# A decoder of six sub-layers on one core: one block of denominators added by GpSimd, other orders in three stages, a split ending

## What is computed

```
x = ln(x + differential_attention(x))     # 16 heads in pairs, out1 - lambda * out2, causal
x = ln(x + long_convolution(x, ctx, ctx)) # 32 groups of 8 channels, filter as long as the sequence
x = ln(x + experts(x))                    # top 2 of 8
x = ln(x + attention(x))                  # "P": plain, 16 heads of 32, causal
x = ln(x + cross_attention(x, ctx))       # "C": one head, keys are the context and x
x = ln(x + shared_key_attention(x))       # "H" then "A": 16 heads, one shared key and value
```

## Time and profile before

| | us |
|---|---|
| three runs | 2245.63, 2247.85, 2248.08 (median 2247.85) |
| the profiled execution | 2249.93 |
| its span (first to last instruction) | 2248.10 |
| PE busy | 2099.8 (93% of the span) |
| DVE busy | 1248.4 (56%) |
| POOL busy | 546.9 (24%) |

### The profile page before, as it was taken

One profiled execution on the slowest core, in us unless ns is written; L12 is line 12 of the kernel. 1 busy time (PEld: TensorE's weight loads), 2 busy tenths in 40 slices (PEclk: granted clock), 3 DMA queues, 4 the chain that ended last, 5 costly groups with the idle time before them and its releaser, 6 DMA issues. The chain is left out here.

```text
span 2248.1 us, 29336 instructions
## 1 busy us (share of the span) xinstructions
PE 2099.8 (93%) x11903; PEld 1226.3 (55%) x11903; DVE 1248.4 (56%) x1886; ACT 517.0 (23%) x783; POOL 546.9 (24%) x514
## 2 busy tenths in 40 slices
PE   6899999888999899899999879999999999999996
PEld 4444444333444466565565646566666666666653
DVE  2467777666999944022222234355757585847465
ACT  1444444440000121111111111222222222222221
POOL 2122222227777400011111310212221212111122
PEclk9999999989999999999999989999999999999997
DMA  9850000005111045412221520101010101010000
GB/s 175 98 41 29 29 29 20 31 19 193 41 41 48 28 145 213 171 66 66 66 66 60 202 76 29 48 1 48 1 57 1 57 1 38 1 29 10 1 10 20
DMA packets 65634, 129.58 MB, mean 58 GB/s; under 512 B 6400, under 2 KB 19840, under 8 KB 65504
## 3 DMA queue, kind: packets, MB, share of 16 engines
q1 hardware_dynamic: 44848, 75.39, 13.3%
q10 hardware_dynamic: 14976, 33.69, 4.1%
q0 software_dynamic: 5680, 18.62, 2.8%
HBM read 96.36 MB, written 41.81 MB: 61 GB/s over the span
## 5 line engine op out<-in xcount | busy, mean ns | idle before, releaser
L930 PE MATMUL conv_conv<-kv,toep 128*128 128x512 f32 x576 | 248.6, 594 | 0.0
L2267 DVE RECIPROCAL tail_inv<-tail_ring 128x256 f32<-128x256 f32 x64 | 112.4, 1757 | 179.8 <-PE tail_ring L1729 179.6
L1428 PE MATMUL moe_gu_ps<-gu,moe_xT 128*128 x624 | 199.8, 463 | 3.9 <-issue 2.3
L930 PEld LDWEIGHTS conv_conv<-kv,toep 128*128 128x128 f32 x576 | 108.7, 191 | 140.5 <-issue 124.4
L953 POOL TENSOR_TENSOR kv<-vT,cT 128x512 f32<-128x512 f32 x128 | 147.8, 1176 | 57.7 <-PE conv_conv L930 53.1
L1428 PEld LDWEIGHTS moe_gu_ps<-gu,moe_xT 128*128 128x128 f32 x624 | 116.4, 192 | 73.2 <-issue 24.2
L2012 POOL TENSOR_TENSOR tail_rstd_x<-tail_rstd_x,const_minus_half 128x2 f32<-128x2 f32 x32 | 22.6, 708 | 481.5 <-DVE tail_rstd_x L2219 481.5
L2019 POOL TENSOR_SCALAR_AFFINE_SELECT tail_expT<-tail_expT 128x1024 f32<-128x1024 f32 x64 | 71.2, 1113 | 276.0 <-ACT tail_expT L2089 275.3
L540 POOL TENSOR_SCALAR_AFFINE_SELECT front_expT<-front_expT 128x2048 f32<-128x2048 f32 x32 | 64.4, 2013 | 259.9 <-ACT front_expT L598 259.9
L1512 DVE TENSOR_TENSOR moe_hid<-moe_gu_ps,moe_silu 128x352 f32<-128x352 f32 x39 | 20.5, 525 | 180.0 <-PE moe_gu_ps L1428 180.0
L2089 ACT ACTIVATE tail_expT<-tail_scores 128x1536 f32<-128x1536 f32 x64 | 92.9, 1451 | 74.6 <-PE tail_scores L1707 74.6
(11 more groups left out here) (349 smaller groups left out, 3968.3 us busy)
## 6 DMA issues: line engine op xcount, KB each, us to landing
toep<-toeplitz SPq DMA_DIRECT2D x32, 320.0 KB, 2.9
y_slots<-moe_y ACTq DMA_DIRECT2D x39, 256.0 KB, 2.0
gu<-in_L_ffn_gate_up_proj SPq DMA_DIRECT2D x5, 1408.0 KB, 10.5
toeplitz<-filt_rows SPq DMA_DIRECT2D x1, 6144.0 KB, 67.1
front_e<-in_ctx SPq DMA_DIRECT2D x8, 512.0 KB, 5.9
toeplitz<-filt_rows SPq DMA_DIRECT2D x2, 2048.0 KB, 88.2
x_after<-x SPq DMA_DIRECT2D x8, 512.0 KB, 5.0
tail_x<-x_after SPq DMA_DIRECT2D x8, 512.0 KB, 3.7
```

Source lines behind the costliest of these rows:

```text
L930: ins = pe.matmul(bank, toep[p][:, mat * P:(mat + 1) * P], kv[p][:, c].rearrange("p b j i -> p (b j i)"), start=n == 0, stop=n == len(PART ...
L1428: ins = pe.matmul(gu_ps[:, s % 2, h, 0:HID], xT[:, c, :], wgu[c][:, e, h * HID:(h + 1) * HID], start=c == 0, stop=c == NC - 1)
L2267: link.after(dve.reciprocal(inv[c % 2][:], bank[:, S:2 * S]))
```

## The change

It has five parts.

1. First stage, denominators: for f = 0 to 6 GpSimd adds the exponentials of key blocks n = 4 and n = 5 into block 5 (`sum_keys`, 128x2048 f32, in place), once O(f, 1, 1) has been computed from them, and Z(f, 1, 1) then has 4 matmuls instead of 8 and waits for this sum.
2. First stage, order: value(d) moves ahead of score(a, 3), Z and the context's transposes behind it, square_sums(f, 1) behind score(a, 5), on VectorE combine(f, 1, 1) behind maxima(a, 3). Round 1 (a = 0) gets an order of its own, with a projection behind each score block. The four loads of `wo` move on ScalarE's queue behind take_value(0).
3. Convolution: the products of two blocks lie side by side, and one `sums` adds both (64 reductions instead of 128).
4. Tail, rounds 0 and 1: written out by hand on TensorE, ScalarE and VectorE, with own query, key and value buffers for sequence 1, and projections and score blocks alternating.
5. Tail, end: for the last A GpSimd adds no blocks (TensorE takes all three), and rows t = 0 and t = 1 are added, normalised and stored one after the other.

```diff
+        def summed_keys(b, ab, t):
+            return ab == t == 1 and b < B - 1
...
                     for name in names:
+                        one = name == "Z" and summed_keys(b, ab, t)
+                        if one:
+                            pe.wait_ge(keys_summed, b + 1)
                         bank = ring.claim(pe, (name, b, ab, t))
-                        for kt in range(t + 1):
+                        for kt in range(t if one else 0, t + 1):
...
                         if f is not None: weigh(f, 1, 1, ("O",))
+                        if a == 0: query(d, 1)
                         score(a, 2)
+                        if a == 0: key(d)
+                        if d is not None and a: value(d)
+                        score(a, 3)
+                        if d is not None and a == 0: value(d)
                         if f is not None:
                             weigh(f, 1, 1, ("Z",))
                             turn_context(f)
-                        score(a, 3)
-                        if d is not None: value(d)
                         if u is not None: turn_tokens(u)
                         score(a, 4)
-                        if d is not None: key(d)
+                        if a == 0: query(d, 2)
+                        elif d is not None: key(d)
+                        score(a, 5)
                         if f is not None: square_sums(f, 1)
-                        score(a, 5)
-                        if d is not None:
+                        if d is not None and a:
                             query(d, 1)
                             query(d, 2)
...
+                def sum_keys(b):
+                    key = ("O", b, 1, 1)
+                    pool.wait_ge(ring.filled_sem(key), ring.count(key))
+                    first, second = (exp_buf(b, n)[:].rearrange("p g j q -> p (g j q)") for n in (4, 5))
+                    pool.tensor_tensor(second, first, second, ALU.add).then_inc(keys_summed, 1)
+
                 for r, d, a, f, u in rounds():
+                    if f is not None and f < B - 1: sum_keys(f)
                     if f is not None: add_eps(f, 1)
...
                     if a is not None: maxima(a, 2)
-                    if f is not None: combine(f, 1, 1)
-                    if a is not None: maxima(a, 3)
+                    if f is not None and a is None: combine(f, 1, 1)
+                    if a is not None:
+                        maxima(a, 3)
+                        if f is not None: combine(f, 1, 1)
```

The convolution's VectorE list, of which `weighted` is L994 before, `completed` L999 and the products L1001:

```diff
                 for h in range(H):
...
+                    weighted(h, 0)
+                    weighted(h, 1)
+                    taken(h, 1)
+                    sums(h, 0, 2)
+                    taken(h, "both")
+                    if h < H - 1:
+                        completed(h, 2)
+                        completed(h, 3)
+                        taken(h, 3)
+                        for lc in (2, 3):
+                            ins = dve.tensor_tensor(total[:, lc - 2], total[:, lc - 2], context_of(lc, h, 2), ALU.mult)
+                        link.after(ins)
+                        sums(h, 2, 2)
```

The end of the tail's hand-written round 1 on VectorE:

```diff
+                cross_rows(0, 1)
+                dve.wait_ge(ring.drained_sem(("C", "w", 0, 1)), ring.count(("C", "w", 0, 1)))
+                norm("x3", 2)
+                statistics("x5", 0)
+                mix("P", 1, 3)
+                add_plain(1)
```

More of the change, by code:

```diff
@@ L621, in _ @@
                 take_value(0)
+                for g in range(4):
+                    act.dma_start(wo[32 * g:32 * g + 32], wo_rows[g]).then_inc(wo_loaded, 16)
                 act.wait_ge(half_made, 6)
@@ L641, in _ @@
                     if d is not None: take_query(d, 0)
+                    if a == 0:
+                        take_query(d, 1)
+                        take_key(d)
+                    if d is not None and d:
+                        take_value(d)
                     if f is not None:
@@ L657, in _ @@
                         act.activation(warm[:], half[:, 0:1], ACT.Exp)
[L658 removed]
+                    if d is not None and a != 0:
                         take_query(d, 1)
@@ L1812, in _ @@
                 ctx_queries(B - 1)
-                for r in range(B):
+                turn("P", "x3", 0)
+                pe.wait_ge(loaded["wq"], 16)
+                turned("P", 0)
+                cols("P", "q", 0, 0, wide["wq"])
+                pe.wait_ge(loaded["wk"], 16)
+                cols("P", "k", 0, 0, wide["wk"])
+                score("P", 0, 0)
+                cols("P", "q", 0, 1, wide["wq"])
+                score("P", 0, 1)
+                cols("P", "k", 0, 1, wide["wk"])
@@ new lines, in _ @@
+                score("P", 0, 2)
+                pe.wait_ge(loaded["wv"], 16)
+                rows("P", "v", 0, 0, xT[0], wide["wv"])
+                score("P", 0, 3)
+                rows("P", "v", 0, 1, xT[0], wide["wv"])
+                turn("P", "x3", 1)
+                turned("P", 1)
+                cols("P", "q", 1, 0, wide["wq"])
+                pe.wait_ge(made, 2)
+                pe.wait_ge(pick_made, 9)
+                shift("P", 0)
+                cols("P", "k", 1, 0, wide["wk"])
@@ new lines, in _ @@
+                pe.wait_ge(loaded["wo"], 16)
+                for n in range(NC):
+                    drained(("P", "W", 0, n))
+                for t in range(NT):
+                    rows("P", "o", 0, t, mixedT, wide["wo"])
+                score("P", 1, 0)
+                ctx_values(B - 1, 1)
+                turn("C", "x4", 0)
+                turned("C", 0)
+                rows("C", "v", 0, 0, xT[0], wvo)
+                score("P", 1, 1)
+                rows("C", "v", 0, 1, xT[0], wvo)
@@ L1814, in _ @@
+                cross_out(0, 0)
+                weigh("P", 1, 2)
+                cross_out(0, 1)
+                weigh("P", 1, 3)
+                for n in range(NC):
+                    drained(("P", "W", 1, n))
+                for t in range(NT):
+                    rows("P", "o", 1, t, mixedT, wide["wo"])
+                for r in range(2, B):
                     p, c, h, a = (r - n if 0 <= r - n < B else None for n in range(4))
@@ L2063, in _ @@
                         causal("A", b, n)
-                root("x6", B - 1)
+                for t in range(NT):
+                    pool.wait_ge(var_ready["x6"], B + t)
+                    rows = rstd["x6"][:, t:t + 1]
+                    pool.tensor_tensor(rows, rows, consts["minus_half"][:, 0:1], ALU.pow).then_inc(rstd_ready["x6"], 1)
             @block.scalar
@@ L2123, in _ @@
+                exps("P", 1, 2)
+                take(("C", "p", 0, 1), probT[:, 1].rearrange("p k q -> p (k q)"))
+                exps("P", 1, 3)
+                for r in range(2, B):
                     p, c, h, a = (r - n if 0 <= r - n < B else None for n in range(4))
```

247 lines of the change are left out of this document (186 added, 61 removed).

## The result

The changed kernel takes 2269.28 us (median of four runs, 2267.11 to 2269.50) against 2247.97 for the kernel before, measured again beside it: 1.0088 times as long, with a 95% interval of 1.0073 to 1.0102. It is slower by 21 us where 16 were forecast. The profiled execution spans 2267.6 us (before 2248.1).

A forecast was written before the change was run, and what follows sets the result against it. TensorE was the engine to watch, with little to take in the first stage, more in the tail's first rounds. 41.4 - 3.3 - 1.5 - 4 - 14 - 2.3 = +16.3 gave 2264 us, range 2237 to 2274.

The forecast's parts named there:

- the hold: Full first-stage rounds: GpSimd's 4.5 us addition blocks VectorE's two skip products, so score block 3 starts 3.6 us later.
- Rival 2: First stage: the addition does not hold back VectorE's skip products, rounds cost +2.4 us; median 2237; chance 0.18.
- Rival 1: First stage: the addition blocks but the clock stays up, 5.5 us less, 2258; chance 0.20.
- rival 3: Blocking as forecast, but tail returns all clock and waits (-24), addition short (2.0): 2240 to 2244; chance 0.09.
- rival 4: First stage: the clock falls in every full round for longer (+2.5 us or more each): 2272; chance 0.08.
- the banks: Full first-stage rounds: the new order makes TensorE wait 1.9, 0.5 and 0.9 us against 0.93 saved, +2.4 a round.
- the clock: Full first-stage rounds: TensorE's clock falls after the waits, taken as +1.1 us a round (bounds 0 and 2.5).
- round 8: First stage, no projections, VectorE sets the pace: the blocked skip products pass on whole, +3.5 us.
- round 2: First stage, no skip products there: the round costs +2.4 us.
- Start: Round 1 and start: projections fill waits, -3.3 us; other loads leave the value weights' way, -1.5.
- Convolution: End of the convolution stage: with half the reductions VectorE keeps up; -4 us, collisions with GpSimd remaining.
- Tail: Rounds 0 and 1: waits 8.9 us less, half of the clock's 13.9 back, less 2: -14 (bounds -6 and -24).

The follow-up runs named there:

- e2: The changed kernel with VectorE's two skip products moved behind the maxima of block 2, GpSimd's addition kept: 2241.5 us (0.9964).
- e1: The changed kernel without GpSimd's addition, Z with its 8 matmuls again, all orders as changed: 2241.4 us (0.9966).
- e6: e2 with the key projection ahead of the context's transposes, the tokens' transposes behind score block 4: 2231.9 us (0.9925).
- e3: The changed kernel with GpSimd's addition cut into four pieces of 512 elements: 2247.07 us (0.9993).
- e4: The changed kernel with parts 1 and 2 undone in the first stage's rounds 2 to 8, the rest kept: 2226.53 us (0.9896).
- e7: e4 with mix 3 ahead of the norm of x3 and the statistics of x5 at the end of the tail's round 1: 2220.74 us (0.9873).
- e10: e7 with the old convolution stage (128 reductions, one block each): 2222.57 us (two runs; 0.9891).
- e8: e7 with the norm of x4 ahead of the maxima of P's score block 0 in the tail's round 1: 2220.17 us (0.9878).
- e9: e7 with the four loads of wo back at the head of ScalarE's queue: 2230.21 us (three runs; 0.9922).

## Why the prediction was right, and where its sizes were off

The forecast was 2264, with 2254 to 2274 as its own range, and 2269.28 was measured. The stated range of 2237 to 2274 also held the opposite outcome, so it says little; what bears the prediction out is the full round. That rounds 3 to 7 meet the forecast to 0.1 us is chance (hold, clock and order are each off by 0.1 to 0.3 a round and cancel), and in the rest of the sum misses of up to 4.8 us partly cancel.

**Right: the hold.** The addition was forecast at 4.5 us, starting just ahead of the skip products, which would take about 5; measured are 4.51, 0.38 ahead, 5.34. The wait before block 3 was forecast at 4.2 and is 3.80 with 0.15 more of wake-up. Block 3 starts 3.4 us later than in e2, counted from the end of block 2 (5.85, e2 2.49), where 3.6 was forecast. The Trainium skill, "SBUF — State Buffer", section "Who interferes with whom", says that a VectorE instruction with two SBUF inputs contends with a GpSimd instruction that reads SBUF, and calls the port pair that they share an exclusive lock. The longest products agree with it (4.68 us where one alone takes 0.74), and so do the maxima of e2, which are not held. Source line of the skip products, lowest, median and highest duration in ns:

```profile
L764 DVE SCALAR_TENSOR_TENSOR front_skipped<-front_x,front_skips,front_e x2: 739/2710/4680, 400.9 to 405.5; 128x512 f32<-128x512 f32 x2
```

Rival 2 (the addition does not block) would have been e2's or e1's time: 2241, where it said 2237. Rival 1 (the clock stays up) falls by block 3's 2.98 us, rival 3 by the addition's 4.51, and rival 4 by the clock's price of 1.4 a round, under its 2.5.

**Right: the banks.** Waits of 1.9, 0.5 and 0.9 were forecast, net +2.4 a round. Measured are 1.46 (1.49 in e2), 0.43 (round 2 and e2) and 0.62, each with 0.17 of wake-up in e2: 3.1 in all, less 0.85 of Z (1.85 before, 1.00 in e2), is the +2.3 between e2 and before. e6 shows that the first of them is for O's bank.

**Right: the clock.** +1.1 a round was forecast. e3 and e2 show its part: without the long wait block 3 takes 1.61 us from start to next start, with it 2.98, which is 1.4 more. Hold and clock together are 4.7 as forecast (3.6 + 1.1), by 3.4 + 1.4.

**Too small: round 8, +3.5 against +8.3.** The step "the blocked skip products pass on whole" stopped at the block of 3.6. Timeline of the changed kernel there:

```profile
465.28 5.67 DVE L764 SCALAR_TENSOR_TENSOR front_skipped<-kept_wa,front_skips,front_e 128x512 f32<-128x512 f32 x2
...
465.91 4.50 POOL L565 TENSOR_TENSOR front_expT<-front_expT 128x2048 f32<-128x2048 f32 x1 [8.50 <-PE front_ring L379]
...
473.21 1.03 PE L319 MATMUL front_scores<-const_mask_bf,const_ident_bf 128*128 128x256 bf16 x4 [5.81 <-DVE front_negtop L709]
474.18 2.09 PE L323 MATMUL front_scores<-front_kT,front_qT 32*128 32x512 f32 x8
...
485.33 1.89 PE L327 MATMUL front_scores<-const_mask_bf,const_ident_bf 128*128 128x512 bf16 x4 [2.48 <-DVE front_negtop L713]
487.14 1.92 PE L331 MATMUL front_scores<-front_kT,front_qT 32*128 32x256 f32 x16
```

VectorE had got one product through, and the second waited 4.3 us all the same. TensorE, with no projections, then waits 5.81 us, and blocks 3 and 5 both run at half clock (2.99 and 3.66 where full clock takes 1.6 and 2.0): 4.3 + 1.4 + 1.6 are 7.3 of the 8.3. Where VectorE sets the pace the clock costs time too, since each block's time is in the chain.

**Too large: round 2, +2.4 against 0.** The score part is 1.65 longer (21.17, was 19.52). In the trace of before the output projection behind it ran at a lower clock (5.17 us instead of 3.70), here not. This is no accident of one trace: round 2 takes 57.3 us, that loss included, in each of before, e4 and e7 to e10, which have the old order there, and in none of the changed kernel and e1 to e3 is the projection slow. So the new order gave the clock back what it took in waits; why it does is not shown, and the prediction, which had no clock term in round 2, could not have said it.

**Start: a term mis-sized, and hidden again.** For the loads -1.5 was forecast; the first values start 5.5 earlier (9.21, were 14.67) and the wait fell to 1.44. Of it 3.0 reach the first score block, which starts at 26.91, since the projections then ran in part at half clock (queries 8.86 us, before 7.17). The round's chain gave 3.5 (forecast 3.3), and half-clock blocks behind it took 3.3 back. In e1, e3, e8 and e10, with the same instructions, round 1's tokens are turned at 23.5 to 24.1 instead of 26.04, and in these four and e2 round 2 begins at 76.8 to 78.5 instead of 81.52. The same instructions thus gained 3.3 us here and 6.3 to 8.0 there (forecast 4.8), by the clock that they drew.

**Convolution: -4 against -2.3.** The step that failed is "with half the reductions it keeps up". A sum over two blocks takes 1.22 us where two sums took 1.37, so the reductions save 9.6 us in the stage. The products of two SBUF tensors take them back: beside GpSimd's `kv` they now need 1.37 us each instead of 1.13, nearly twice the 0.69 of a free one, 11.7 more in all. VectorE is busy 241.6 us in the stage where it was 239.5. Groups of instructions in the stage (busy us, mean ns of one, idle before), first before, then after the change:

```profile
L986 DVE TENSOR_REDUCE vT<-prod 128x64 f32<-128x512 f32 x128 | 87.8, 686 | 4.4
L1001 DVE TENSOR_TENSOR prod<-total,cT 128x512 f32<-128x512 f32 x64 | 72.4, 1131 | 2.2
```

```profile
L1038 DVE TENSOR_TENSOR total<-total,cT 128x512 f32<-128x512 f32 x62 | 82.7, 1372 | 1.1
L1025 DVE TENSOR_REDUCE vT<-prod 128x128 f32<-128x1024 f32 x32 | 39.0, 1220 | 1.1
```

The prediction had allowed 1.2 us for such collisions (-5.2 to -4). That the products are held by GpSimd fits the first stage, and that their new place, two in a row, is what lengthens them is argued, not shown. In the last group VectorE is busy with the first pair until 807.77, and then stand two additions, two products and two sums, 4.1 us, not three instructions. Timeline, changed kernel:

```profile
806.55 1.22 DVE L1025 TENSOR_REDUCE vT<-prod 128x128 f32<-128x1024 f32 x1
807.69 0.68 DVE L1020 TENSOR_TENSOR total<-conv_conv,both 128x512 f32<-128x512 f32 x1
...
812.57 3.64 PE L1123 MATMUL midl_ring<-const_ident,vT 128*128 128x128 f32 x16 [5.85 <-PEq L52]
```

**Tail: -14 against -12.8, the waits right, the clock a draw.** The waits were to fall by 8.9 to 15.4; they stand at 15.4 and fell by 8.1, since 23.5 is what they were. The new one is 4.67 (forecast 4.9), the one among the transposed blocks 3.31 (3); that the rest meets the sum is luck, as before cross attention they are 3.1 (2.30 + 0.77) where 4.5 were forecast. The other 5.1 were "of the clock's 13.9 I take half back, less 2", and there the step fails: the same instructions, with the same waits, take 143.40 us here and 147.08 to 147.16 in each of e1 to e6. Against 156.15 that is -12.8 and -9.0 for one program: hardly more than the waits in six traces, and 3.7 more of clock in one. The forecast of -14 fits the one, and the six are 5 short of it. With mix 3 first it is 139.4 and 139.7 in e8 and e7, 143.4 in e9 and e10. The 2.8 us in a later round are of this kind: a matmul group (`tail_gk`) there took 3.73 us before and takes 2.01 now; the granted clock of the 12.17 and 9.40 us around it is 0.72 and 1.00.

**End: right.** The addition's place in the last chain gives 1.15 (69.89 us from the last transposes of tokens to those of the last output, was 71.04), the split 0.9.

**What nobody gains.** The halved Z saved 5.9 us of TensorE's work (0.85 each of seven) and the first stage has no place to put them: VectorE's maxima set the distance of the score blocks, 2.4 us with wake-ups, and the work between them was 2.78, 2.77 and 2.69 us before, just enough. e6 fills the gaps better than the changed kernel and still is 1.0 a round above the old order. That no order can profit is argued, not shown.

## What to carry to other kernels

Before an elementwise instruction is given to GpSimd, look up what VectorE does in its whole length: with two SBUF inputs it will stand still, with its input in PSUM, like the maxima here, it will not, and one line moved on VectorE was worth 28 us. If no clean place exists, cut the instruction in pieces (22 us here). In the convolution longer products beside GpSimd used up all the time that the paired reductions saved on VectorE. Where blocks alternate between two engines, work taken out of a full gap turns into a wait, and a wait behind which the clock falls costs about 1.4 us more at the next block. The same program also drew clocks that put one stretch 3.7 us apart, so a gain in a stage with waits should be read over several traces.

## What the hardware showed that I had not expected

- Between two queued GpSimd instructions the held VectorE instruction gets its turn: four additions of 512 elements need 5.82 us with VectorE's products between them, and these end after 3.10.
- A wait of 1.56 us before a score block left its clock up (mask 0.61 us), one of 3.80 did not (1.04), in the same place of the same round.
